# A keys pass whose turned blocks go from SBUF to SBUF by sixteen transfers, without a store to DRAM and four loads

## What is computed

```
xn = layernorm(x)
q, k, v = xn @ wq, xn @ wk, xn @ wv            # per head: 32 columns
pk = exp(k' @ omega.T - 0.5 |k'|^2 - max) / sqrt(128) + 1e-6     # k' = k * 32**-0.25
kv = sum over rows of pk^T v,   z = sum over rows of pk
```

## Time and profile before

| what | us |
|---|---|
| median of three runs (3192.41 to 3194.93) | 3194.19 |
| the profiled execution, its own time | 3190.72 |
| its span, first to last instruction | 3188.9 |
| PE busy in the span | 3125.2 |
| SP's DMA issues in the span (count) | 1579 |

### The profile page before, as it was taken

One profiled execution on the slowest core, in us unless ns is written; L12 is line 12 of the kernel. 1 busy time (PEld: TensorE's weight loads), 2 busy tenths in 40 slices (PEclk: granted clock), 3 DMA queues, 4 the chain that ended last, 5 costly groups with the idle time before them and its releaser, 6 DMA issues.

```text
span 3188.9 us, 71767 instructions
## 1 busy us (share of the span) xinstructions
PE 3125.2 (98%) x27633; PEld 2770.3 (87%) x27633; DVE 2290.8 (72%) x4582; ACT 1644.1 (52%) x3560; POOL 1028.1 (32%) x828
## 2 busy tenths in 40 slices
PE   8999999997999999999999999999999999999998
PEld 6888888886878787777777799999999999999998
DVE  6888888886666666666666666666766766767666
ACT  5677777764555454554555544444444444444443
POOL 2455544544555565565656310000000000000000
PEclk9999999998999999999999999999999999999999
DMA  7666666654354544444444665444445554444454
GB/s 227 202 188 194 201 187 200 197 189 101 90 156 115 144 126 131 125 134 123 138 135 117 201 218 171 157 163 158 152 161 166 167 171 159 160 165 148 160 169 133
DMA packets 450307, 510.17 MB, mean 160 GB/s; under 512 B 298800, under 2 KB 323888, under 8 KB 449968
## 3 DMA queue, kind: packets, MB, share of 16 engines
q1 hardware_dynamic: 449968, 505.59, 51.0%
HBM read 342.83 MB, written 162.66 MB: 159 GB/s over the span
## 4 chain that ended last, share of the span: by engine, by line
PE 55%; POOL 10%; DVE 3%; issue 3%; ACT 3%; DMA 2%; SPq 1%; ACTq 0%; DVEq 0%; POOLq 0%
PE ffn_hidden L188 29%; PE shared_bank L188 12%; PE ffn_result L188 7%; POOL shared_y L1209 3%; PE attend_feat L1372 2%; POOL shared_y L1207 2%; POOL attend_oT_lo L1191 2%; PE attend_num L1410 2%; PE attend_turn L1410 2%; POOL attend_ka_lo L1187 1%; POOL shared_mix_lo L1183 1%; DMA ffn_r_in<-r_d 1%; DVE ffn_yb L1834 1%; ACT attend_act_k L1252 1%; ACT attend_ka_hi L1256 1%
## 5 line engine op out<-in xcount | busy, mean ns | idle before, releaser
L188 PE MATMUL ffn_hidden<-ffn_yT_hi,ffn_wa_hi 128*128 128x256 f32 x2048 | 572.6, 280 | 2.5 <-DVE ffn_wa_lo L1755 2.5
L188 PE MATMUL ffn_hidden<-ffn_yT_lo,ffn_wa_hi 128*128 128x256 f32 x2048 | 573.6, 280 | 0.0
L188 PE MATMUL ffn_hidden<-ffn_yT_hi,ffn_wa_lo 128*128 128x256 f32 x2048 | 572.2, 279 | 0.0
L333 POOL TENSOR_TENSOR ffn_n_rstd<-ffn_n_base,ffn_n_power 128x2 f32<-128x2 f32 x32 | 27.5, 860 | 1274.7 <-DVE ffn_n_negmean L328 1274.7
L188 PEld LDWEIGHTS ffn_hidden<-ffn_yT_hi,ffn_wa_hi 128*128 128x128 f32 x2048 | 385.6, 188 | 3.4 <-DVE ffn_wa_lo L1755 2.7
L188 PEld LDWEIGHTS ffn_hidden<-ffn_yT_hi,ffn_wa_lo 128*128 128x128 f32 x2048 | 385.7, 188 | 0.0
L188 PEld LDWEIGHTS ffn_hidden<-ffn_yT_lo,ffn_wa_hi 128*128 128x128 f32 x2048 | 385.3, 188 | 0.2
L1737 ACT ACTIVATE ffn_ht_hi<-ffn_hs 128x512 fp32r<-128x512 f32 x248 | 156.3, 630 | 426.0 <-DVE ffn_hs L1784 426.0
L728 ACT ACTIVATE keys_e<-keys_feat,keys_below 128x128 f32<-128x128 f32 x1024 | 273.0, 436 | 187.0 <-DVE keys_below L811 187.0
L655 POOL TENSOR_TENSOR keys_z_sum<-keys_z_sum,keys_e 128x512 f32<-128x512 f32 x192 | 262.5, 1397 | 257.0 <-ACT keys_e L728 257.0
L1788 DVE TENSOR_TENSOR ffn_ht_lo<-ffn_hs,ffn_ht_hi 128x512 fp32r<-128x512 f32 x248 | 173.7, 700 | 218.7 <-ACT ffn_ht_hi L1737 218.7
(11 more groups left out here) (306 smaller groups left out, 9218.2 us busy)
## 6 DMA issues: line engine op xcount, KB each, us to landing
ffn_tq<-part_d SPq DMA_DIRECT2D x248, 512.0 KB, 5.1
keys_xin<-in_L_attn_x_dram SPq DMA_DIRECT2D x32, 512.0 KB, 4.3
xn_d<-keys_xn SPq DMA_DIRECT2D x32, 512.0 KB, 5.2
xt_d<-keys_xn_turned SPq DMA_DIRECT2D x32, 512.0 KB, 2.7
keys_xT_whole<-xt_d SPq DMA_DIRECT2D x128, 128.0 KB, 3.2
xT_d<-keys_xT_whole SPq DMA_DIRECT2D x32, 512.0 KB, 3.9
kt_d<-keys_uk_turned SPq DMA_DIRECT2D x32, 512.0 KB, 3.5
keys_kT<-kt_d SPq DMA_DIRECT2D x128, 128.0 KB, 3.4
```

What stands on the lines that cost most here:

```text
L188: last = pe.matmul(out, stationary[a], moving[b], start=start and n == 0, stop=stop and n == len(TERMS) - 1)
```

## The change

A function `put_turned` takes the place of the store and `load_turned` in the keys pass. It issues sixteen DMAs from SBUF to SBUF, one for each (a, b), each from 32 partitions to 32 partitions, with 4 pieces of 256 bytes per partition (128 pieces, 32 KB). The DRAM tensors `xt_d` and `kt_d` go. The pairs of jobs become one job each, "xt" and "kt". What waited for a store (`xt_stored`, `kt_stored`) now waits for the sixteen transfers (`xt_loaded`, `k_loaded`, 256 instead of 64 per group and buffer): on DVE these are turn_x and turn_k, which write over the turned tile. "xt" stands at lead 3, where "xt_out" stood, with "whole" right behind it.

```diff
+def put_turned(sp, dst, src, loaded):
+    for a in range(HC):
+        for b in range(HC):
+            sp.dma_start(dst[b * KD:(b + 1) * KD, :, a * KD * TG:(a + 1) * KD * TG],
+                         src[a * KD:(a + 1) * KD, b:H:HC, :, :].rearrange("p c k t -> p c (k t)"))\
+                .then_inc(loaded, 16)
...
-        SP_BODY = [("u", 0, 0), ("xt_in", 0, 2), ("kt_out", 0, 1), ("kt_in", 0, 1), ("whole", 0, 2), ("sums", 0, -1),
-                   ("x", 0, 4), ("xn", 0, 3), ("xt_out", 0, 3)]
+        SP_BODY = [("u", 0, 0), ("kt", 0, 1), ("sums", 0, -1),
+                   ("x", 0, 4), ("xn", 0, 3), ("xt", 0, 3), ("whole", 0, 3)]
...
-                if job == "xt_out":
+                if job == "xt":
                     wait_alone(sp, x_turned, TG * g + TG, sp_passed)
-                    sp.dma_start(xt_d[g], xn_turned[:, :, :, :].rearrange("p b j t -> p b (j t)")).then_inc(xt_stored, 16)
-                if job == "xt_in":
-                    sp.wait_ge(xt_stored, 16 * g + 16)
                     wait(sp, x_split, 2 * (g - 1))
                     if g > 1:
-                        wait_alone(sp, xT_stored, 16 * (g - 1), sp_passed)
-                    load_turned(sp, xT_whole[g % 2], xt_d[g], xt_loaded[g % 2])
+                        wait_alone(sp, xT_stored, 16 * g, sp_passed)
+                    put_turned(sp, xT_whole[g % 2], xn_turned, xt_loaded[g % 2])
                 if job == "whole":
-                    wait_alone(sp, xt_loaded[g % 2], 64 * (g // 2 + 1), sp_passed)
+                    wait_alone(sp, xt_loaded[g % 2], 256 * (g // 2 + 1), sp_passed)
...
-                if job == "kt_out":
+                if job == "kt":
                     wait_alone(sp, k_turned, TG * g + TG, sp_passed)
-                    sp.dma_start(kt_d[g], uk_turned[:, :, :, :].rearrange("p b j t -> p b (j t)")).then_inc(kt_stored, 16)
-                if job == "kt_in":
-                    wait_alone(sp, kt_stored, 16 * g + 16, sp_passed)
                     for j in range(HC):
                         wait(sp, feat[j].full, TG * (g - 1))
-                    load_turned(sp, kT[g % 2], kt_d[g], k_loaded[g % 2])
+                    put_turned(sp, kT[g % 2], uk_turned, k_loaded[g % 2])
...
                 if job == "turn_x":
-                    wait(dve, xt_stored, 16 * g)
+                    wait(dve, xt_loaded[(g - 1) % 2], 256 * ((g + 1) // 2))
```

More of the change, by code:

```diff
@@ L370 @@
 SP_KEYS_END = (("next", "w", 0, 0), ("next", "w", 1, 0), ("next", "w", 2, 0), ("keys", "u", 0, -2),
-               ("keys", "kt_out", 0, -1), ("keys", "kt_in", 0, -1), ("next", "w", 3, 0), ("next", "w", 4, 0),
+               ("keys", "kt", 0, -1), ("next", "w", 3, 0), ("next", "w", 4, 0),
                ("keys", "u", 0, -1), ("next", "x", 0, 0), ("next", "mu", 0, 0), ("next", "w", 5, 0),
@@ L374, with keys_pass @@
                ("keys", "sums", 0, -1))
-def keys_pass(nc, places, shared, shared_banks, early, wo, w_r, w_k, w_v, mu_r, mu_k, x, wq, wk, wv, omega, xn_d, xT_d, xt_d, kt_d, u_d, kv_d, n_batches, groups_per_batch):
+def keys_pass(nc, places, shared, shared_banks, early, wo, w_r, w_k, w_v, mu_r, mu_k, x, wq, wk, wv, omega, xn_d, xT_d, u_d, kv_d, n_batches, groups_per_batch):
     G = n_batches * groups_per_batch
@@ L444, in keys_pass @@
         first_turned, x_split = sem("first_turned"), sem("x_split")
-        x_turned, xt_stored, xt_loaded = sem("x_turned"), sem("xt_stored"), [sem(f"xt_loaded{n}") for n in range(2)]
-        k_turned, kt_stored, k_loaded = sem("k_turned"), sem("kt_stored"), [sem(f"k_loaded{n}") for n in range(2)]
+        x_turned, xt_loaded = sem("x_turned"), [sem(f"xt_loaded{n}") for n in range(2)]
+        k_turned, k_loaded = sem("k_turned"), [sem(f"k_loaded{n}") for n in range(2)]
         v_added = sem("v_added")
@@ L516, in keys_pass @@
                      ("z", 6, 0), ("z", 7, 0)]
-        SP_BODY = [("u", 0, 0), ("xt_in", 0, 2), ("kt_out", 0, 1), ("kt_in", 0, 1), ("whole", 0, 2), ("sums", 0, -1),
-                   ("x", 0, 4), ("xn", 0, 3), ("xt_out", 0, 3)]
+        SP_BODY = [("u", 0, 0), ("kt", 0, 1), ("sums", 0, -1),
+                   ("x", 0, 4), ("xn", 0, 3), ("xt", 0, 3), ("whole", 0, 3)]
         HEAD = [("x", 0, 0), ("stats", 0, 0), ("half", 0, 0), ("weights", 0, 0), ("norm", 0, 0), ("half", 1, 0), ("first", 0, 0), ("first", 1, 0),
-                ("x", 0, 1), ("xn", 0, 0), ("turn_x", 0, 0), ("xt_out", 0, 0), ("xt_in", 0, 0), ("stats", 0, 1),
[1 row of a table added]
                 ("weights", 1, 0), ("k", 0, 0), ("norm", 0, 1), ("xn", 0, 1), ("x", 0, 2), ("turn_x", 0, 1),
                 ("weights", 2, 0), ("k", 1, 0), ("turn_k", 0, 0), ("sq", 0, 0), ("turn_k", 1, 0), ("sq", 1, 0),
-                ("xt_out", 0, 1), ("xt_in", 0, 1), ("whole", 0, 0), ("kt_out", 0, 0), ("kt_in", 0, 0), ("whole", 0, 1),
[1 row of a table added]
                 ("q", 0, 0), ("stats", 0, 2), ("q", 1, 0), ("split", 0, 1), ("split", 1, 1), ("norm", 0, 2), ("x", 0, 3),
                 ("xn", 0, 2), ("v", 0, 0), ("v_out", 0, 0), ("v_sum", 0, 0), ("turn_q", 0, 0), ("turn_q", 1, 0),
-                ("turn_x", 0, 2), ("xt_out", 0, 2), ("v", 1, 0), ("v_out", 1, 0)]
+                ("turn_x", 0, 2), ("xt", 0, 2), ("whole", 0, 2), ("v", 1, 0), ("v_out", 1, 0)]
         def run(eng, do, order, head=HEAD):
@@ L621, in _ @@
             sp.wait_ge(xn_stored, 16 * G)
-            sp.wait_ge(xt_stored, 16 * G)
-            sp.wait_ge(kt_stored, 16 * G)
+            for n in range(2):
+                sp.wait_ge(xt_loaded[n], 256 * (G // 2))
+                sp.wait_ge(k_loaded[n], 256 * (G // 2))
             sp.wait_ge(xT_stored, 16 * G)
@@ L695, in do @@
                 if job == "split":
-                    act.wait_ge(xt_loaded[g % 2], 64 * (g // 2 + 1))
+                    act.wait_ge(xt_loaded[g % 2], 256 * (g // 2 + 1))
                     for t in range(TG):
@@ L778, in do @@
                     dve.wait_ge(k_free[n], g + 1)
-                    wait(dve, kt_stored, 16 * g)
+                    wait(dve, k_loaded[(g - 1) % 2], 256 * ((g + 1) // 2))
                     dve.transpose(uk_turned[:, :, :, n], uk[:, n, :].rearrange("p (b k) -> p b k", k=KD)).then_inc(k_turned, 1)
@@ L895, in do @@
                 if job == "proj":
-                    pe.wait_ge(k_loaded[g % 2], 64 * (g // 2 + 1))
+                    pe.wait_ge(k_loaded[g % 2], 256 * (g // 2 + 1))
                     wait(pe, e_ready[1 - n], NC * g + NC if n == 1 else NC * g)
@@ L1975, in performer_and_gated_block @@
     xT_d = nc.dram_tensor("xT_d", [n_groups, P, NC, GT], FP32, kind="Internal").ap()
-    xt_d = nc.dram_tensor("xt_d", [n_groups, P, H, KD * TG], FP32, kind="Internal").ap()
-    kt_d = nc.dram_tensor("kt_d", [n_groups, P, H, KD * TG], FP32, kind="Internal").ap()
     u_d = nc.dram_tensor("u_d", [n_groups, P, H, KD * TG], FP32, kind="Internal").ap()
@@ L1995, in performer_and_gated_block @@
     shared_banks = [nc.alloc_psum_tensor(f"shared_bank{n}", [P, W], FP32) for n in range(TG)]
-    keys_pass(nc, keys_places, shared, shared_banks, early, wo, w_r, w_k, w_v, mu_r, mu_k, x_rows, wq, wk, wv, omega, xn_d, xT_d, xt_d, kt_d, u_d,
+    keys_pass(nc, keys_places, shared, shared_banks, early, wo, w_r, w_k, w_v, mu_r, mu_k, x_rows, wq, wk, wv, omega, xn_d, xT_d, u_d,
               kv_d, B, S // GT)
```

## The result

The change makes the kernel slower: 3340.86 us (median of 4 runs, 3337.75 to 3343.01) against 3193.3 us in the runs of before beside it, a ratio of 1.0459 with a 95% interval of 1.0446 to 1.0471, 147.6 us. The prediction was no change, 3194 us with 3189 to 3215. What happened is its first rival: SP becomes the bound.

The account below looks back on a forecast made before the run. PE's own work was taken as the bound, with SP fitting at 19.9 of 21.9 us per body. 0 us in the steady part and -0.3 us in the head gave 3194 us against 3194.19, range 3189 to 3215.

Parts of the forecast that it names:

- Rival 1: SP's queue, keys pass: issues make SP the bound, from 0.54 us each; about 3320 us at 0.65; chance 0.19.
- The bound: Keys pass, 80 to 690 us: PE's own work sets the time, busy 608.40 of 610 us; SP is the engine loaded.
- What goes and what is left of SP: SP per body: 6.4 us of x and k stores and loads go, plus two store waits; 3.1 us of work are left.
- What comes: SP per body: 32 issues at 0.475 us, 15.2 us, plus 1.55 us standing for a landing; SP's sum 19.9 of 21.9.
- The break-even: SP in a body: the price per issue from which SP becomes the bound, 0.54 us.
- the deadlines inside a body: Steady part, with 0.475 per issue and landing 2.0: all met, narrowest margin 1.8 to 2.0 us, PE loses 0 us.
- the ends 0.43 and 0.65: SP's price per issue in us: below, an issue with nothing added; above, a quarter of four loads of 512 pieces.
- The head: Start of the keys pass, second group's `xT`: landed 34.4 where ACT had it at 34.67, -0.3 us.
- a way that the prediction had set aside: DVE at the start: low halves of wv queue behind turn_x's wait; PE was said to stand later in any case.
- DVE's waits: DVE in a body: added waits of turn_x and turn_k are met 10 and 4 us ahead; 0 us for PE.
- the last rival: Keys pass transfers: they run one after another, each with its whole landing; about 3950 us; chance 0.01.

Follow-up runs that it names:

- shared4: The whole change, but SP issues twelve of each block's sixteen transfers and POOL the other four, against the changed kernel; 3191.98 us, ratio to before 1.0006.

## Why the prediction was wrong

- **The bound.** PE at 608.40 of 610, and SP as the engine to watch: right.
- **What goes and what is left of SP.** 3.1 us left of the work, 1.55 us of wait for the landing. Measured 27.24 - 11.69 - 11.83 - 1.36 = 2.4 us in the body shown (1.36 is its wait for the landing) and 33.0 / 22 = 1.5 us. Both near enough.
- **What comes: the failed step.** 0.475 us per issue was the rate of loads from DRAM. It is right for those (0.47 again by itself), but a transfer from SBUF to SBUF costs 0.65 in a quiet queue, 0.70 on the mean of the pass and 0.73 in the body shown. The sum was 19.9 us; with 0.70 and its other terms unchanged it is 3.1 + 1.55 + 32 x 0.70 = 27.1, and the mean body measured 26.8. The break-even was put at 0.54, so the wrong side followed from this term alone; the deadlines inside a body, worked out with 0.475, fell with it.
- **How the step was chosen.** Between the ends 0.43 and 0.65 I went by the number of pieces, as the nearest likeness. From SBUF to SBUF four pieces instead of one count for 0.02 us; the same pattern loaded from DRAM costs 0.18 less. The earlier trace rows had a DMA at 0.56, above the break-even, and I gave it less weight than the earlier trace rows. With both ends so placed around the break-even, a chance of 0.19 and a range that ended at 3215 were too little: the price at the upper end was 3320.
- **Rival 1.** Place and mechanism were right, and that there is a threshold; its size was 3320 at 0.65, against 3341: the long issues put the mean, 0.70, above the upper end. That the upper end was near is luck: it came from loads of 512 pieces, and rows from or to DRAM don't bound a price from SBUF to SBUF.
- **The head.** -0.3 us was predicted; ACT's split of the second group began at 39.25 instead of 34.67, 4.6 us later, from the same price. Rival 1 had 6.4 there at 0.65 and a landing of 2.7; the landing is 1.9. PE's gap did not close (3.99 us for 3.75). And DVE's wait for the first group's transfers reached PE by a way that the prediction had set aside, the low half of wv behind it on DVE; as PE then waited for `xT` again, this added nothing to the 4.6 us (PE in the head, in order of time; brackets: idle before):

```profile
29.87 0.50 PE L197 MATMUL shared_bank<-keys_wv_hi,keys_xT_hi 128*128 128x512 f32 x1 [3.38 <-DVE keys_wv_lo L299]
```

- **DVE's waits and the last rival.** In the steady part DVE's new conditions cost nothing by themselves (shared4 keeps them). And transfers don't run one after another with their landings: sixteen issues and the last landing took 11.83 + 1.36 = 13.2 us in the body shown, where sixteen landings of 1.9 would be 30.4.

## What to carry to other kernels

Count the issues of a queue in a body, multiply them by a price read from a DMA with the same memory at each end, and add the waits that stand between them; when no such row exists, and the bounds lie on both sides of the break-even, forecast by the break-even and not by the likeliest row. Replacing a store and four loads by sixteen copies without HBM moves the cost from the transfer, which was hidden, to the issuing engine, which is serial. If such a queue is just full, give a quarter of the issues to an engine with an idle gap of that size, and see that what stands behind them there is not awaited.

## What the runs showed of the hardware that was not expected

- An issue on SP, in a quiet queue, cost 0.63 to 0.65 us from SBUF to SBUF (32 or 128 rows, 256 B or 1 KB each; 0.71 with 8 rows) and 0.63 from DRAM to DRAM, against 0.47 for loads and 0.48 for plain stores of 128 rows of 1 KB. On POOL, from SBUF to SBUF in pieces, it was 0.55.
- Four pieces per partition raised the price of a store from 0.48 to 0.66 but not that of a load (0.47 with and without); a load with sixteen per partition took 0.65.
- With SP and ACT issuing the same transfers at once, SP's took 3% longer than alone and ACT's 1% (10.47 against 10.38 us).
